# Two small reorderings in a two-layer attention and feed-forward kernel: DVE's order at the start of attention 2, and the last stage's sums handled bank by bank

## The reference, cut to what matters

```
x = x + aft_block(norm(x), ctx)      # local attention-free transformer, then a 256-1024-256 relu MLP
x = x + moe(norm(x))                 # 64 experts of width 64, top 8, plus two shared experts of width 512
x = x + attention(norm(x), ctx, ctx, mask)   # 16 heads of 16: softmax(QK'/4, masked) V, then Wo   ("attention 2")
x = x + mlp(norm(x))                 # binarized: w -> mean|w| * sign(w); gelu; 256-1024-256         ("last stage")
```

## Time and profile before

| | |
|---|---|
| time, median of 3 runs | 1273.25 us (1272.36 to 1275.16) |
| the profiled execution's own time | 1272.18 us |
| its span, first to last instruction | 1270.5 us |
| PE busy | 1142.3 us, 90% |
| DVE busy | 878.1 us, 69% |
| ACT busy | 703.6 us, 55% |
| POOL busy | 343.7 us, 27% |
| mean granted TensorE clock | 0.979 of full speed |

### The profile page before, as it was taken

One profiled execution on the slowest core, in us unless ns is written; L12 is line 12 of the kernel. 1 busy time (PEld: TensorE's weight loads), 2 busy tenths in 40 slices (PEclk: granted clock), 3 DMA queues, 4 the chain that ended last, 5 costly groups with the idle time before them and its releaser, 6 DMA issues. The chain is left out here.

```text
span 1270.5 us, 19924 instructions
## 1 busy us (share of the span) xinstructions
PE 1142.3 (90%) x6928; PEld 997.4 (79%) x6928; DVE 878.1 (69%) x1653; ACT 703.6 (55%) x1063; POOL 343.7 (27%) x343
## 2 busy tenths in 40 slices
PE   0778899788987999999999989999999999989998
PEld 0557788677877999999999978778788788777887
DVE  3576756766674655655755443999989989997575
ACT  1213323365543444444444233888988988986755
POOL 2520202251170510600600045512442442233120
PEclk9989999899998999999999999999999999998999
DMA  9200000004334444344332023321421423310001
GB/s 313 67 1 1 1 1 1 1 1 137 71 71 112 113 115 138 94 120 134 91 95 54 1 76 100 100 58 59 136 64 54 138 62 119 95 39 5 14 24 48
DMA packets 68967, 92.88 MB, mean 73 GB/s; under 512 B 16016, under 2 KB 33168, under 8 KB 68752
## 3 DMA queue, kind: packets, MB, share of 16 engines
q1 hardware_dynamic: 67264, 89.67, 25.0%
q10 hardware_dynamic: 1616, 2.10, 0.5%
HBM read 80.45 MB, written 11.14 MB: 72 GB/s over the span
## 5 line engine op out<-in xcount | busy, mean ns | idle before, releaser
L1997 DVE CUSTOM_DVE_ANT_0 at_pr<-at_sc,at_mk 128x512 f32<-128x512 f32 x256 | 165.5, 683 | 26.2 <-PE at_sc L2228 25.7
L1901 ACT ACTIVATE at_pr<-at_pr,at_nmx 128x512 f32<-128x512 f32 x256 | 170.5, 717 | 17.8 <-DVE at_nmx L1997 17.2
L2139 DVE TENSOR_TENSOR W_1l<-at_pt,W_1h 128x1024 fp32r<-128x1024 f32 x128 | 155.8, 1218 | 6.1 <-ACT W_1h L1896 5.7
L1896 ACT ACTIVATE W_1h<-at_pt 128x1024 fp32r<-128x1024 f32 x128 | 130.8, 1022 | 34.7 <-PE at_o L2262 33.2
L2243 PE MATMUL at_pt<-ident,at_pr 128*128 128x128 f32 x1024 | 135.2, 275 | 15.0 <-DVE W_1l L2139 14.2
L2243 PEld LDWEIGHTS at_pt<-ident,at_pr 128*128 128x128 f32 x1024 | 115.3, 142 | 38.4 <-issue 17.0
L228 ACT ACTIVATE moe_hs<-moe_hid,cols 128x512 f32<-128x512 f32 x120 | 82.8, 690 | 100.4 <-PE moe_hid L114 99.5
L247 DVE TENSOR_TENSOR moe_hl<-moe_ms,moe_hh 128x512 fp32r<-128x512 f32 x104 | 80.4, 773 | 64.3 <-ACT moe_hh L220 64.3
L261 DVE TENSOR_TENSOR moe_ms<-moe_hs,gate 128x512 f32<-128x512 f32 x104 | 78.7, 757 | 57.4 <-ACT moe_hs L228 57.0
L220 ACT ACTIVATE moe_hh<-moe_ms 128x512 fp32r<-128x512 f32 x104 | 65.8, 633 | 94.2 <-DVE moe_ms L261 94.2
L2262 PE MATMUL at_o<-W_1h,at_vaug 128*128 128x512 f32 x256 | 112.1, 438 | 0.3 <-DVE W_1l L2139 0.3
(11 more groups left out here) (304 smaller groups left out, 3304.2 us busy)
## 6 DMA issues: line engine op xcount, KB each, us to landing
gate<-expert_weights SPq DMA_DIRECT2D x256, 128.0 KB, 3.0
w_stage<-in_ew SPq DMA_DIRECT2D x32, 256.0 KB, 4.0
at_kp<-at_heads SPq DMA_DIRECT2D x96, 64.0 KB, 2.7
at_qp<-at_heads SPq DMA_DIRECT2D x96, 64.0 KB, 2.8
w_stage<-in_mask SPq DMA_DIRECT2D x16, 256.0 KB, 3.6
at_rb<-at_recip SPq DMA_DIRECT2D x64, 64.0 KB, 2.1
w_stage<-in_w SPq DMA_DIRECT2D x8, 256.0 KB, 7.3
w_stage<-in_sw SPq DMA_DIRECT2D x8, 256.0 KB, 3.3
```

What stands on the lines that cost most here:

```text
L1896: act.activation(PH[0][:, n % 2, :], PT[n % 2][:, :, :].rearrange("p c q -> p (c q)"), ACT.Copy)\
L1901: act.activation(pr_of(t)[:, x, :], pr_of(t)[:, x, :], ACT.Exp, bias=nmx[:, t % 4, x:x + 1], scale=-1.0).then_inc(s["ex"], 1)
L1997: dve.tensor_tensor_reduce(pr_of(t)[:, x, :], SB[x][:, :], mk[u // 2 % 2][:, j, :], -float(HD) ** -0.5, 3.0e38, ALU.add, ALU.min, nmx[:, t ...
L2139: dve.tensor_tensor(PH[1][:, n % 2, :], PT[n % 2][:, :, :].rearrange("p c q -> p (c q)"), f(PH[0][:, n % 2, :]), ALU.subtract).then_inc(s[ ...
```

## The change

Three edits, all in `attention_phase`:

1. DVE, unit -1, step 3: `low_turn(0)` is issued ahead of the weights' low part instead of behind it. Step 4's `low_turn(1)` stays where it was.
2. PE gets a new semaphore `fy0`, raised by the fourth of the eight output matmuls of a batch's last tile, when bank 0 is complete. DVE's scale of bank 0 waits for `fy0`, that of bank 1 for `fy` as before. For the last batch DVE now does scale 0, add 0, scale 1, add 1 instead of scale 0, scale 1, add 0, add 1. For the batches before, the order stays scale, scale, low part, add, add.
3. SP stores each batch in two halves of 256 KB, each after its own add, instead of one store of 512 KB; the final wait counts 32 per batch.

```diff
@@ names of semaphores
-             "flo", "fy", "fb2", "ffin", "fout", "stored")
+             "flo", "fy", "fy0", "fb2", "ffin", "fout", "stored")
@@ SP
             def store_out(b):
-                sp.wait_ge(s["fout"], 2 * b + 2)
-                sp.dma_start(g.out.rearrange("(t p) d -> p t d", p=P)[:, b * TT:(b + 1) * TT, :],
-                             g.x_res[:, b * TT:(b + 1) * TT, :]).then_inc(s["stored"], 16)
+                for j in range(2):
+                    part = slice(b * TT + 2 * j, b * TT + 2 * j + 2)
+                    sp.wait_ge(s["fout"], 2 * b + j + 1)
+                    sp.dma_start(g.out.rearrange("(t p) d -> p t d", p=P)[:, part, :], g.x_res[:, part, :])\
+                      .then_inc(s["stored"], 16)
...
-            sp.wait_ge(s["stored"], 16 * B)
+            sp.wait_ge(s["stored"], 32 * B)
@@ DVE
-            def ffn_scale(b):
-                dve.wait_ge(s["fy"], HT * b + HT)
+            def ffn_scale(b, banks=(0, 1)):
                 if b:
                     dve.wait_ge(s["fout"], 2 * b)
-                for j in range(2):
+                for j in banks:
+                    if j == 0:
+                        dve.wait_ge(s["fy0"], b + 1)
+                    else:
+                        dve.wait_ge(s["fy"], HT * b + HT)
                     dve.tensor_tensor(fin[:, j], YO[j].rearrange("p (t d) -> p t d", d=D), tiles(alpha2[:, :]), ALU.mult)\
                         .then_inc(s["ffin"], 1)
...
-            def ffn_add(b):
+            def ffn_add(b, banks=(0, 1)):
...
                     if u == -1:
+                        if st in (3, 4):
+                            low_turn(st - 3)
                         if st == 3:
                             dve.wait_ge(s_wh, 1)
                             dve.tensor_tensor(WP[1][:, :, :, :], wst, f(WP[0][:, :, :, :]), ALU.subtract).then_inc(s_wl, 1)
-                        if st in (3, 4):
-                            low_turn(st - 3)
...
-            ffn_scale(B - 1)
-            ffn_add(B - 1)
+            for j in range(2):
+                ffn_scale(B - 1, (j,))
+                ffn_add(B - 1, (j,))
@@ PE, ffn_output
+                    if t == HT - 1 and tt == 1:
+                        last.then_inc(s["fy0"], 1)
                 last.then_inc(s["fy"], 1)
```

## The result

Eleven runs of the changed kernel have a median of 1269.09 us (1266.59 to 1273.22), eleven of the kernel before 1274.68 us. The ratio is 0.996, with a 95% interval of 0.9945 to 0.9975: 5.1 us or 0.40% less, with 3.2 to 7.0 us as ends. The forecast was 1269.3 us and a gain of 3.91 us (0.31%).

The account below looks back on a forecast made before the run. PE was taken to bound the kernel, working back to back behind attention 2's start, where it waits 2.7 us. Savings 2.68 + 0.25 + 0.18 + 0.8 = 3.91 us take 1273.25 to 1269.3 us; 8-in-10 range 1268.0 to 1271.6.

Parts of the forecast that it names:

- Part 1: Start of attention 2: the turn's low part ahead of the weights' brings the first key product 2.68 us earlier.
- rival (a): Start of attention 2: weights' low part keeps its 2.83 us, key product saves only 2.09, 1269.9 us; chance 0.10.
- The cover: Behind the key product: fifth tail low part, held beside POOL's bias addition, has 0.9 us before PE needs it.
- Part 2: Last change of batch: signal at bank 0 starts DVE's scale half a tile earlier, 0.25 us; nothing at earlier changes.
- Part 3: End of kernel: last add ends 0.18 us earlier, and the last store, 256 KB instead of 512, takes 0.8 less.
- Rival (b): Attention steps from 797 us: the lead is lost again, only parts 2 and 3 remain, 1272.0 us; chance 0.13.
- (c): Last store: the second half store costs what the whole did, a fixed price per store, 1270.1 us; chance 0.05.
- (e): Last batch: bank 0's signal does nothing at all, so 0.25 and 0.47 are gone, 1270.1 us; chance 0.07.
- rival (d): Shifted start of attention 2: granted clock falls there and costs 6.6 us, slower at 1275.9 us; chance 0.02.
- The forecast's own low end: Whole kernel: the smallest saving the forecast allowed, given as 2.63 us, for a time of 1270.6 us.
- The sign that was to prove it wrong: In the trace after: a granted clock of 0.5 in a stretch that had 1.00 means the prediction is wrong altogether.

Follow-up runs that it names:

- ctx_early: The kernel before, with POOL's low part of the context moved ahead of the second pair of clears; ratio to before 0.9991, mean 1274.53 us.
- stats_early: The change with the last batch back to scale, scale, add, add and its norm statistics one step earlier on DVE; ratio to before 0.9937.
- turn_only: The kernel before with only the first turn's low part moved ahead of the weights' low part; ratio to before 0.9974, mean 1271.68 us.
- tail_only: The change with DVE's order of turn and weights' low parts as before, keeping early signal, alternation and half stores; ratio to before 1.0, mean 1274.94 us.
- longer_wait: The kernel before with four more DVE subtractions between the weights' and the first turn's low part; ratio to before 1.0029, mean 1279.15 us.
- before_again: The kernel before, unedited, traced a second time; turn 0 to first key product 9.47 us, against 9.41 in the first trace.
- stores_only: The kernel before with only the stores split in halves; last output matmul's start to the span's end 5.53 us, against 6.15 before.
- after_again: The changed kernel, unedited, traced a second time; turn 0 to first key product 6.74 us, against 6.72; ratio to before again 0.996.

## Why the prediction was right, point by point

- **The number.** That forecast and median agree to 0.2 us is in part luck. Before's own median was 1.43 us higher than the 1273.25 that the forecast started from, and the measured gain was larger than forecast by about as much (5.1 us, 3.2 to 7.0, for 3.91). The distances hold 3.6 us of it; the mechanisms of parts 1 and 2 and of the split store are the ones that were forecast, the alternation is not.
- **Part 1, 2.68 us.** Right in mechanism and size: A fell by 2.69. The weights' part took 2.24 us, near the 2.2 named as the sign, and rival (a), with 2.83, is out. The step that carried it, that a lock against POOL had already delayed the weights' part, was an inference from duration; ctx_early shows it (1.75 us with no subtraction of POOL beside it). This is the rule of the Trainium skill (SBUF — State Buffer, section Who interferes with whom), and the runs agree with it for subtractions; that the turn's low part, with an operand from PSUM, isn't held agrees too (0.68 us at 758.66 while POOL subtracted until 759.88). The key product came 0.1 us later than PE was ready, and B is 0.11 longer; 2.58 of the 2.69 arrive at 797 us.
- **The cover.** The fifth tail low part was held beside the bias addition as foreseen, for 1.93 us, and PE had no wait behind it.
- **Part 2, 0.25 us.** C is 0.21 to 0.25 less in every kernel with the signal and unchanged in every kernel without (stats_early's C is shorter for its other edit too). That the signal does nothing at the change to the third batch, and why, is shown by stats_early; at the change to the second batch PE's wait is 1.05 us before and 1.06 after, so the signal does nothing there either, but its reason was only argued.
- **Part 3, 0.18 and 0.8 us.** Of the 0.98 us, D holds 0.79. The first term was mis-sized: DVE's end gained 0.01, not 0.18. The wait of an add for its own scale is 0.11 (1264.89 to 1265.00) and not 0.06, twice, and the first scale starts 0.41 earlier and not 0.47. Alternation thus gives back all that the signal gains. The store gained 0.78, for 0.8 forecast; but that is worth 0.62 without the spacing that alternation brings, so the two terms were not independent as the sum had them.
- **Sum.** The distances hold 2.58 + 0.25 + 0.79 = 3.6 us for the 3.91 forecast. The forecast's own low end should be 2.09 + 0 + 0.02 + 0.5 = 2.61 us and not 2.63, which changes nothing. Rival (b) is out: B lost 0.11, and from the first score maximum (798.02 and 799.97) to the one-time sums (1159.85 and 1161.72) it is 361.8 us in both. Rivals (c) and (e) are out by D and C.
- **The rest of the measured 5.1 to 5.5.** How the change comes to more clock stays open. The prediction costed the wait at its own length and took the clock as unchanged; rival (d) looked for a change in clock on the wrong side. In the two pairs of traces, the other 1.7 and 1.8 us lie between B's end and C's start, with the clock at half speed for 3.4 us less. Over the runs, the change's clock is 0.0023 above before's, worth 2.7 us by the slope (0.0018 and 2.1 us on the one chip that timed both with clocks). Some of that is plain arithmetic: the stretch at half clock after PE's last work is shorter by the 0.8 us that D lost, which raises the mean by about 0.8 x 0.5 / 1270 = 0.0003. This also brings the -2.8 us at equal clock nearer to the distances' 3.6.
- **Is it the removed wait?** It can be: against before on the same chip, the kernels without the wait have a clock higher by 0.0011 (turn_only), 0.0034, 0.0027, 0.0018 and 0.0010, those with a wait by 0.0003 (ctx_early), -0.0005 (tail_only) and -0.0018 (longer_wait), each within ±0.0009 to 0.0022. How it would act the traces don't show: right behind the wait of 2.7 to 3.0 us one of four has a fall (tail_only; before, before_again and stores_only don't), and the largest differences in time at half speed, 44.4 to 51.2 us, lie ahead of 743 us, where all kernels are the same.
- **The sign that was to prove it wrong**, a granted clock of 0.5 in a stretch that had 1.00, did show at 747 to 750 us in the change's first trace. It stands ahead of the changed code, behind PE's 2.54 us between the two program parts. Of the thirteen traces five have a fall at 746 to 748 us (the change's first, turn_only, ctx_early, stats_early, longer_wait) and eight haven't, among them after_again, though PE's idle time there is 2.5 us in every one. A sign that comes and goes in unchanged code can't judge the change on a single trace.

## What to carry to other kernels

Before a long instruction is moved, its duration is to be compared with what its columns should take; time above that can be a wait for another engine (here it was), and it can shrink or move elsewhere (ctx_early) when the order changes. Splitting the last store pays only as far as its parts are apart in time, and putting dependent instructions next to each other on one engine costs 0.11 us each plus the lost overlap, so an early signal and a new order should be costed together. For effects under 0.3%, distances inside a trace tell more than times, but they must be read beside the stretches that they leave out, where the clock can differ by more than the effect. An idle stretch of PE may also cost clock behind it (5.63 us for 3.31 us of work in longer_wait); how much on average is not settled here.

## What the runs showed of the hardware that had not been expected

- A DVE normalization (tensor_scalar, both ends in SBUF, 128x256) is also held beside POOL's subtractions: four of them took 4.19 us beside two of these and 2.07 in before's trace. A clear on POOL didn't lengthen a DVE subtraction of two SBUF operands (1.75 us for 1536 columns).
- PE's clock was still at 1.00 during an idle stretch of 2.99 us and fell to half speed about 1.4 us after work had started again; in an idle stretch of 5.65 us it fell before its end. At the end of an idle stretch of 2.5 us, or up to about a microsecond and a half behind it, it fell in five traces of thirteen. It stayed low for 3.4 us behind the 2.99 us and for 6.8 with the 5.65, as the shares in the windows give it.
- The mean granted clock of whole runs wanders from 0.973 to 0.981, at 1.18 us for each thousandth. That is most of the spread of a kernel's times: a scatter of 2.3 us falls to 0.78 when it is taken out.
